# Feed-forward of a transformer layer: the gelu of every second tile is split in rows of tokens and turned by a transfer

## The reference

```
x = x + attention(layernorm(x))
h = layer_norm(layernorm(x), ln1_g, ln1_b)
h = einsum('bsd,hd->bsh', h, ternary_quant(w1)) + b1      # 128 -> 512
h = gelu(h, approximate=False)
h = layer_norm(h, ln2_g, ln2_b)                           # over the 512
x = x + einsum('bsh,dh->bsd', h, ternary_quant(w2)) + b2  # 512 -> 128
```

## Time and profile before

| | |
|---|---|
| median of three runs | 1002.18 us |
| profiled execution, span from first to last instruction | 998.7 us |
| TensorE busy | 980.8 us (98%) |
| VectorE busy | 880.0 us (88%) |
| GpSimd busy | 837.1 us (84%) |
| ScalarE busy | 729.6 us (73%) |
| TensorE in the chain that ended last | 95% |
| TensorE clock granted | full in all 40 slices |
| first and last matmul of `f_hidden` | 872.5 and 990.6 us |

### The profile page before, as it was taken

How to read it: one execution, slowest core, us unless ns; L and a number is a source line. 1 busy time by engine, 2 the same in 40 slices (tenths; PEclk the granted TensorE clock), 3 DMA queues, 4 the chain that set the end, 5 groups by cost and what they waited for, 6 DMA issues and landing times.

```text
span 998.7 us, 39391 instructions
## 1 busy us (share of the span) xinstructions
PE 980.8 (98%) x16052; PEld 782.2 (78%) x16052; DVE 880.0 (88%) x1779; ACT 729.6 (73%) x1151; POOL 837.1 (84%) x861
## 2 busy tenths in 40 slices
PE   7899999999999999999999999999999999999998
PEld 6577777778777787887887777888878777788886
DVE  7888988988889888898889988889889988788998
ACT  5687677777767777777777777777777776879995
POOL 6789888989887888888899888888888889866765
PEclk9999999999999999999999999999999999999999
DMA  6112332222331232233222233324222233354343
GB/s 141 38 32 51 53 66 45 43 49 52 74 53 27 51 73 53 52 53 71 55 48 41 48 73 51 53 53 71 46 41 47 52 52 53 69 86 75 77 86 65
DMA packets 203682, 57.82 MB, mean 58 GB/s; under 512 B 185072, under 2 KB 203248, under 8 KB 203504
## 3 DMA queue, kind: packets, MB, share of 16 engines
q1 hardware_dynamic: 201424, 54.79, 29.8%
q10 hardware_dynamic: 2080, 0.52, 0.2%
HBM read 7.21 MB, written 4.19 MB: 11 GB/s over the span
## 4 chain that ended last, share of the span: by engine, by line
PE 95%; DVE 2%; ACT 1%; issue 1%; POOL 1%; DVEq 0%; POOLq 0%; ACTq 0%
PE S L675 11%; PE PV L700 8%; PE M L635 7%; PE PV L702 6%; PE PV L701 6%; PE QK L622 5%; PE QK L623 5%; PE QK L624 5%; PE misc L675 5%; PE S L667 5%; PE S L864 3%; PE M L753 2%; PE M L718 2%; PE M L754 2%; PE M L755 2%; PE misc L667 2%
## 5 line engine op out<-in xcount | busy, mean ns | idle before, releaser
L1210 POOL TENSOR_TENSOR pl<-p 128x1024 f16<-128x1024 f32 x253 | 476.9, 1896 | 39.3 <-ACT p L1000 39.1
L1410 DVE TENSOR_REDUCE negmax<-M 128x4 f32<-128x1024 f32 x252 | 306.8, 1217 | 22.4 <-PE M L635 16.4
L1008 ACT ACTIVATE QKh<-QK 128x512 f16<-128x512 f32 x251 | 149.5, 596 | 155.5 <-PE QK L624 155.3
L1000 ACT ACTIVATE p<-S,s_exp 128x1024 f32<-128x1024 f32 x173 | 192.4, 1112 | 71.8 <-PE S L675 71.2
L700 PEld LDWEIGHTS PV<-V,p 128*128 128x128 bf16 x2048 | 186.8, 98 | 46.4 <-issue 34.5
L700 PE MATMUL PV<-V,p 128*128 128x65 f16 x2048 | 214.9, 194 | 4.0 <-DVE O L1424 2.9
L701 PE MATMUL PV<-V,p 128*128 128x64 f16 x2048 | 213.4, 193 | 0.0
L702 PE MATMUL PV<-V,pl 128*128 128x65 f16 x2048 | 212.6, 194 | 0.0
L1430 DVE TENSOR_TENSOR QKl<-QK,QKh 128x512 f16<-128x512 f32 x251 | 172.4, 687 | 42.2 <-ACT QKh L1008 41.1
L701 PEld LDWEIGHTS PV<-V,p 128*128 128x128 bf16 x2048 | 189.1, 97 | 4.7
L702 PEld LDWEIGHTS PV<-V,pl 128*128 128x128 f16 x2048 | 188.7, 97 | 0.0
(11 more groups left out here) (236 smaller groups left out, 2501.6 us busy)
## 6 DMA issues: line engine op xcount, KB each, us to landing
result<-X SPq DMA_DIRECT2D x15, 256.0 KB, 2.6
X<-in_L_attn_query SPq DMA_DIRECT2D x7, 512.0 KB, 4.8
OT<-O SPq DMA_TRANSPOSE x64, 4.6
shift<-negmax SPq DMA_TRANSPOSE x63, 2.3
O<-in_L_attn_Wk ACTq DMA_DIRECT2D x2, 256.0 KB, 4.3
O<-in_L_attn_Wq SPq DMA_DIRECT2D x2, 256.0 KB, 4.5
O<-in_L_attn_Wv SPq DMA_DIRECT2D x1, 512.0 KB, 3.9
w<-in_L_ffn_w SPq DMA_DIRECT2D x2, 256.0 KB, 5.6
```

Source lines behind the costliest of these rows:

```text
L1000: e.activation(p32[r][:, :, :, :].rearrange("p i m n -> p (i m n)"), score_bank(p)[:, :], ACT.Exp, scale=s_exp[:, :]).then_inc(s_ex, 1)
L1210: e.tensor_tensor(pl[r][:, :, :, :].rearrange("p i m n -> p (i m n)"), p32[r][:, :, :, :].rearrange("p i m n -> p (i m n)"), p_high(r).rea ...
L1410: e.tensor_reduce(dst[:, :, NB * jj:NB * jj + NB], max_bank(p)[:, :].rearrange("p (i t m) -> p i t m", i=2, t=NB), AX.X, ALU.max, negate=T ...
```

## The change

Of the 64 tiles, those with an even number below 60 are now "rows tiles" (30 of them), the others "bank tiles". A bank tile goes as before. For a rows tile the splitting comes before the turning: VectorE casts `a` to a high part in bfloat16 (`f_zrow_high`), GpSimd subtracts it from `a` to a low part (`f_zrow_low`), both in rows of tokens in a buffer `zp`, and one transfer on SP turns both parts at once to `zT` (`turn_z`). TensorE has no transposes for such a tile and reads `zT` in `f_out`, two turns later than for a bank tile (lag 15 for 13). `f_zhi` on ScalarE and `f_zlo` on VectorE fall away for it.

Since a rows tile is not scaled, the bank tiles aren't either: `inv_f1` and `s_f12` go, the root is multiplied by `s_f2` alone, `f_zhi` becomes a plain copy to bfloat16, and `f_zlo` a plain subtraction. The order of the outputs is no longer that of the tiles (`OUT_ORDER`), and waits count by `OUT_NO`. The sums come a turn later (18 for 17).

On GpSimd the cast of y goes: `f_yhi` on ScalarE now does it for all groups. GpSimd keeps y's low part (`f_ylow`), one turn later. The bias is added to four tiles in one instruction of 512 elements, in the turn of the root (`f_bias`).

```diff
-L_BIAS, L_HID, L_ZT, L_OUT, L_SUM = 14, 10, 11, 13, 17
+L_BIAS, L_HID, L_ZT, L_OUT, L_OUT_ROWS, L_SUM = 6, 10, 11, 13, 15, 18
+ROWS_END = NT - 4
...
+def in_rows(i):
+    return i % 2 == 0 and i < ROWS_END
...
+def out_turn(i):
+    return i + (L_OUT_ROWS if in_rows(i) else L_OUT)
+OUT_ORDER = sorted(range(NT), key=lambda i: (out_turn(i), i))
+BANKS = [i for i in range(NT) if not in_rows(i)]
+OUT_NO = {i: n + 1 for n, i in enumerate(OUT_ORDER)}
+FIRST_OUT = {min(range(FG * g, FG * g + FG), key=OUT_NO.get): g for g in range(NT // FG)}
+LAST_OUT_NO = {g: max(OUT_NO[i] for i in range(FG * g, FG * g + FG) if i != NT - 1) for g in range(NT // FG)}
...
-        zTh = [sb(f"zTh{i}", [P, FC, P], F16) for i in range(3)]
+        zTh = [sb(f"zTh{i}", [P, FC, P], BF16) for i in range(3)]
         zTl = [sb(f"zTl{i}", [P, FC, P], F16) for i in range(3)]
+        zp = [sb(f"zp{i}", [P, 2, FC, P], F16) for i in range(2)]
+        zT = [sb(f"zT{i}", [P, 2, FC, P], F16) for i in range(3)]
...
+            def turn_z(i):
+                n = rows_no(i)
+                e.wait_ge(s_zrlo, n + 1)
+                if n >= 3:
+                    e.wait_ge(s_f, OUT_NO[i - 6])
+                e.dma_start_transpose(zT[n % 3][:, :, :, :].rearrange("p s c n -> p (s c) n"),
+                                      zp[n % 2][:, :, :, :].rearrange("p s c n -> p (s c n)")).then_inc(zt_in[n % 3], 16)
...
+                if u is not None and 0 <= u - L_ZT < NT and in_rows(u - L_ZT):
+                    turn_z(u - L_ZT)
...
             def f_out(i):
                 g, k = divmod(i, FG)
-                e.wait_ge(s_zlo, i + 1)
-                if i == 0:
-                    e.wait_ge(s_qklo, NP)
-                elif i == FG:
-                    e.wait_ge(s_o, NP)
-                elif k == 0:
-                    e.wait_ge(s_out, FG * (g - 1))
+                if in_rows(i):
+                    n = rows_no(i)
+                    e.wait_ge(zt_in[n % 3], z_turned(n))
+                    zh, zl = zT[n % 3][:, 0, :, :].bitcast(BF16), zT[n % 3][:, 1, :, :]
+                else:
+                    n = banks_no(i)
+                    e.wait_ge(s_zlo, n + 1)
+                    zh, zl = zTh[n % 3], zTl[n % 3]
+                if i in FIRST_OUT:
+                    if g == 0:
+                        e.wait_ge(s_qklo, NP)
+                    elif g == 1:
+                        e.wait_ge(s_o, NP)
+                    else:
+                        e.wait_ge(s_out, FG * (g - 1))
...
+                if 0 <= u - L_HID < NT:
+                    f_hidden(u - L_HID)
+                if 0 <= u - L_ZT < NT and not in_rows(u - L_ZT):
+                    f_zT(u - L_ZT)
+                for i in OUT_ORDER:
+                    if out_turn(i) == u and i < NT - 1:
+                        f_out(i)
+                if u == out_turn(NT - 1):
                     f_out_last(NT - 1)
...
             def f_gelu(i):
                 e.wait_ge(s_pre, i + 1)
                 if i >= A_RING:
-                    e.wait_ge(s_zt, i - A_RING + 1)
+                    if in_rows(i - A_RING):
+                        e.wait_ge(s_zrlo, rows_no(i - A_RING) + 1)
+                    else:
+                        e.wait_ge(s_zt, banks_no(i - A_RING) + 1)
                     e.wait_ge(s_st2, i - A_RING + 1)
                 e.activation(a[i % A_RING][:, :], pre_bank[i % 2], ACT.Gelu, scale=s_f1[:, :]).then_inc(s_a, 1)
             def f_zhi(i):
-                e.wait_ge(s_zt, i + 1)
-                if i >= 3:
-                    e.wait_ge(s_f, i - 2)
-                e.activation(zTh[i % 3][:, :, :], z_bank[i % 2][:, :].rearrange("p (c n) -> p c n", c=FC),
-                             ACT.Identity, scale=inv_f1[:, :]).then_inc(s_zhi, 1)
+                n = banks_no(i)
+                e.wait_ge(s_zt, n + 1)
+                if n >= 3:
+                    e.wait_ge(s_f, OUT_NO[BANKS[n - 3]])
+                e.activation(zTh[n % 3][:, :, :], z_bank[n % 2][:, :].rearrange("p (c n) -> p c n", c=FC),
+                             ACT.Copy).then_inc(s_zhi, 1)
...
+                    f_y(u)
+                if u % FG == FG - 1 and u < NT:
                     f_yhi(u // FG)
...
-                e.tensor_scalar(rs2[k][:, :], r2[k][:, :], s_f12[:, :], None, ALU.mult).then_inc(s_rs2, 1)
-            def f_ysplit(g):
-                e.wait_ge(s_y1, FG * g + FG)
-                e.wait_ge(yt_in[g % 2], 16 * (g // 2))
-                e.tensor_copy(yp[g % 2][:, :, 0, :], y[g % 2][:, :, :]).then_inc(s_yhi, 1)
+                e.tensor_scalar(rs2[k][:, :], r2[k][:, :], s_f2[:, :], None, ALU.mult).then_inc(s_rs2, 1)
+            def f_zrow_low(i):
+                n = rows_no(i)
+                e.wait_ge(s_zrhi, n + 1)
+                e.tensor_tensor(z_rows_low(n), a[i % A_RING][:, :], z_rows_high(n), ALU.subtract).then_inc(s_zrlo, 1)
+            def f_ylow(g):
                 e.wait_ge(s_yhi, g + 1)
                 e.tensor_tensor(yp[g % 2][:, :, 1, :], y[g % 2][:, :, :], yp[g % 2][:, :, 0, :],
                                 ALU.subtract).then_inc(s_ylo, 1)
-            def f_bias(i):
-                e.wait_ge(s_y1, i + 1)
-                e.tensor_tensor(X[:, i, :], X[:, i, :], bias2[:, :], ALU.add).then_inc(s_xb, 1)
+            def f_bias(g):
+                e.wait_ge(s_y1, FG * g + FG)
+                tiles = X[:, FG * g:FG * g + FG, :]
+                e.tensor_tensor(tiles, tiles, bias2[:, :].unsqueeze(1).to_broadcast([P, FG, D]), ALU.add).then_inc(s_xb, 1)
...
-                if u % FG == FG - 1 and Y_EARLY <= u // FG < NT // FG:
-                    f_ysplit(u // FG)
-                if u == L_BIAS:
-                    e.wait_ge(s_w, W_AT["bias2"])
-                if 0 <= u - L_BIAS < NT - FG:
-                    f_bias(u - L_BIAS)
-                if u - L_BIAS == NT - FG - 1:
-                    for i in range(NT - FG, NT):
-                        f_bias(i)
+                if 0 <= u - L_ZT < NT and in_rows(u - L_ZT):
+                    f_zrow_low(u - L_ZT)
                 if (u - L_ZT) % FG == FG - 1 and 0 <= u - L_ZT < NT:
                     f_root((u - L_ZT) // FG)
+                if u % FG == 0 and Y_EARLY <= u // FG - 1 < NT // FG:
+                    f_ylow(u // FG - 1)
+                if u == L_BIAS + FG:
+                    e.wait_ge(s_w, W_AT["bias2"])
+                if u % FG == 2 and 0 <= (u - L_BIAS) // FG - 1 < NT // FG:
+                    f_bias((u - L_BIAS) // FG - 1)
...
             def f_zlo(i):
-                e.wait_ge(s_zhi, i + 1)
-                if i >= 3:
-                    e.wait_ge(s_f, i - 2)
-                e.scalar_tensor_tensor(zTl[i % 3][:, :, :], z_bank[i % 2][:, :].rearrange("p (c n) -> p c n", c=FC),
-                                       inv_f1[:, :], zTh[i % 3][:, :, :], ALU.mult, ALU.subtract).then_inc(s_zlo, 1)
+                n = banks_no(i)
+                e.wait_ge(s_zhi, n + 1)
+                if n >= 3:
+                    e.wait_ge(s_f, OUT_NO[BANKS[n - 3]])
+                e.tensor_tensor(zTl[n % 3][:, :, :], z_bank[n % 2][:, :].rearrange("p (c n) -> p c n", c=FC),
+                                zTh[n % 3][:, :, :], ALU.subtract).then_inc(s_zlo, 1)
+            def f_zrow_high(i):
+                n = rows_no(i)
+                e.wait_ge(s_a, i + 1)
+                if n >= 2:
+                    e.wait_ge(zt_in[(n - 2) % 3], z_turned(n - 2))
+                e.tensor_copy(z_rows_high(n), a[i % A_RING][:, :]).then_inc(s_zrhi, 1)
             def f_sum(i):
                 g, k = divmod(i, FG)
-                e.wait_ge(s_f, NT if i == NT - 1 else min(FG * g + FG, NT - 1))
-                e.wait_ge(s_xb, i + 1)
+                e.wait_ge(s_f, NT if i == NT - 1 else LAST_OUT_NO[g])
+                e.wait_ge(s_xb, g + 1)
...
+                if 0 <= u - L_ZT < NT and in_rows(u - L_ZT):
+                    f_zrow_high(u - L_ZT)
                 for i in tiles:
                     f_stats(i)
-                last_turns = u - L_ZT >= NT - 2
-                if 0 <= u - L_SUM < NT and not last_turns:
-                    f_sum(u - L_SUM)
+                for i in sums_in(u):
+                    f_sum(i)
                 for i in tiles:
                     f_variance(i)
-                if 0 <= u - L_ZT < NT:
+                if 0 <= u - L_ZT < NT and not in_rows(u - L_ZT):
                     f_zlo(u - L_ZT)
-                if u - L_ZT == NT - 1:
-                    for i in range(NT - 2 + L_ZT - L_SUM, u - L_SUM + 1):
-                        f_sum(i)
-                if u - L_ZT >= NT:
-                    f_sum(u - L_SUM)
+                for i in last_sums_in(u):
+                    f_sum(i)
```

More of the change, by code:

```diff
@@ L236, in value_order, with rows_no, banks_no, sums_in @@
             yield from two_values(t)
+def in_rows(i):
+    return i % 2 == 0 and i < ROWS_END
+def rows_no(i):
+    return i // 2
+def banks_no(i):
+    return sum(not in_rows(k) for k in range(i))
+def out_turn(i):
```

(42 more changed lines are left out.)

26 lines of the change are left out of this document (10 added, 16 removed).

## The result

| | before | after |
|---|---|---|
| median of four runs | 1002.28 us (1001.26 to 1003.38) | 1009.44 us (1005.37 to 1010.35) |
| ratio | | 1.0071, 95% interval 1.006 to 1.0083 |
| profiled execution, span | 998.7 us | 1003.6 us |

The forecast was 999.7 us. The change makes the kernel slower, beyond the range given. After is profiled in the fastest of its four executions, 1005.37 us; its time is 1.8 over its span, and for the other three only spans of 1007.2 to 1008.5 and a mean granted clock of 0.995 (profiled: 0.997) are known. So a trace can explain 4.9 us of difference (1003.6 against 998.7); the rest of the 7.2 between the medians has no trace. Run again beside the first experiments (e1), after had 1005.86.

A forecast was written before the change was run, and what follows sets the result against it. TensorE bounds the kernel before; after, GpSimd sets a group at 6.34 + 0.6 = 6.95 us against 7.02. 12 x 0.07 = 0.8 plus 1.7 early gives 2.5 us: span 996.2, time 999.7, range 992.5 to 1005.5.

The forecast's parts named there:

- TensorE, 6.15 us a group: Steady stretch: with transposes gone for 30 of 64 tiles, TensorE's work per group of four tiles falls to 6.15 us.
- Early tiles, 1.7 us gained: Tiles 4 to 10, where TensorE is full and VectorE has room: four tiles without transposes gain 1.7 us.
- ScalarE 5.9, VectorE 5.6 to 6.2: Work per group: ScalarE falls from 6.56 to 5.9 us; VectorE has 5.6 to 6.2 before any waiting for GpSimd.
- GpSimd's sum, 6.34: GpSimd's work per group: root 1.75, bias 1.27, y's low part 1.12, two low parts of z 2.20, together 6.34 us.
- the port's 0.6: Port shared by VectorE and GpSimd: each cast holds GpSimd 0.3 us, twice a group, raising 6.34 to 6.95.
- Rival 1: Cast does not hold the port; the chain aggregate, root, bias, low part, transpose sets 6.5 a group: 994.2 us, chance 0.27.
- Rival 2: Cast stalls VectorE behind long GpSimd instructions, lengthening the chain through root and bias: group 7.2 to 7.35, 1005.6 us, chance 0.28.
- the signs named for it: Profile after: a group over 7.1 us with VectorE idle before the cast or TensorE waiting for sums.
- Queues, counted 0: SP and transfer engines: two more transposes a group cost 0; 6.2 us a group of transfer use would fit under 6.95.
- Rival 3: Z's transfer lands too late (4.7 us, not 3.1) or makes no difference; groups 7.1 to 7.3 if everywhere: 1002, chance 0.05.
- The span otherwise unchanged: Outside the early tiles and 12 steady groups nothing was changed in the 998.7 us span; the tail counted 0.
- The 3.5 us around the span: Before's median, 1002.18, is 3.5 us above its profiled span; this was left as it is, giving 999.7 from 996.2.

The follow-up runs named there:

- e1: The changed kernel run once more, unchanged: 1005.86 us, ratio 1.0045 to before.
- e5: The changed kernel with the bias one turn later on GpSimd, behind the low part of z instead of ahead of it: 1001.59 us, ratio 1.0001 to before.
- e9: The changed kernel with VectorE's cast written as a maximum over an axis of length one: 1005.01 us, ratio 1.0049 to before.
- e4: The changed kernel with the cast of the rows tiles on ScalarE instead of VectorE: 1003.39 us, ratio 1.0021 to before.

## Why the prediction was wrong

- **TensorE, 6.15 us a group.** Right as work: the shortest groups of after take 6.14. It never sets the pace for long.
- **Early tiles, 1.7 us gained.** Wrong: 0.7 lost. VectorE had room, but the chain through GpSimd was what ended last, and the bias in it costs 2.2 there (e5).
- **ScalarE 5.9, VectorE 5.6 to 6.2.** Near: 6.07 and 6.07 of 7 us, in groups of 7.1.
- **GpSimd's sum, 6.34, and the port's 0.6.** This is the main failure. The sum itself was right: from start to start the root takes 1.73, the bias 1.23, the two low parts of z 1.12 and 1.13 and y's 1.12 (1.32 less its hold), 6.33 in all. But the port's hold falls mostly on VectorE, and GpSimd pays 0.2 in the group measured, not 0.6: 6.53, not 6.95. That the mean comes near (7.14) is accident: I had named GpSimd's sum as what sets a group, and a ring sets it. The ring stood in rivals 1 and 2 (root, bias, low part, transposes), at 6.5 and 7.2. Rival 2 came nearest, in size (1005.6, against 1005.37 profiled), in the early tiles and in the signs named for it: TensorE waiting, VectorE held up. But its reason, the held cast, isn't shown to be the decisive one: the even casts of e9 left the mean group as it was, and moving the bias (e5) won more than moving the cast (e4).
- **Queues, counted 0.** Wrong. By busy share the transfer engines had room (0.78, or 5.5 us of 7, under the 6.2 allowed for). But SP needs 1.23 to 1.29 us for each issue, y's goes ahead of z's, the transposes land at 3.3 on the median and up to 5.1 instead of the 3.1 of the earlier trace rows, and those with a code load beside them are a microsecond later. Rival 3, at a chance of 0.05, was this.
- **The span otherwise unchanged.** Wrong by 2.7 us at the start and 0.6 at the end, more than the groups lost (1.4). It was set down as an assumption, without a bound. The 3.5 us around the span were wrong too: they are 1.8, so before's profiled execution was itself 1.7 faster than its median.
- **The span's miss added up.** 1003.6 instead of 996.2: 2.7 at the start, 2.4 in the early tiles, 2.2 in the 12 groups, 0.6 at the end, and 0.4 less in the last tiles. So of the 7.4 us the groups, on which nearly all of the working was spent, are under a third.
- **Two slips in the rivals.** Rival 1's 1.64 a turn is 6.6 a group, not 6.5. Rival 3's 7.1 to 7.3 doesn't follow from its own term: 1.6 us more on the chain of 7.4 is 2.0 a turn, or 8.0 a group.

What stays open: the other 2.3 us between the medians, in executions without a trace (their mean clock of 0.995 against 0.997 says that some of it may be clock, no more); why the input lands later; and why the end is 0.6 longer.
